# Normalising attention from PSUM: no copy on ScalarE, attention product eight units later, new unit tables

## The chip, the cores and the metric

One core of one Trainium2 chip runs the whole kernel. The metric is the device time of one execution in microseconds, the median of several runs. Engines: TensorE (PE, its weight loads PEld), VectorE (DVE), ScalarE (ACT), GpSimd (POOL) and SyncE (SP), which issues most DMAs.

## The reference

Eight sequences x of 512 tokens by 512 channels go through one post-norm block, all in float32.

```python
q = x @ Wq                # 16 heads of 32
k, v = x @ Wk, x @ Wv     # 4 heads of 32, each serves 4 query heads
attn = softmax(q @ k.T / sqrt(32))
x = layernorm(x + (attn @ v) @ Wo)
x_scale = max(abs(x)) / 127          # per token; weights likewise per output, int8
y = (round(x / x_scale) @ w_int8.T) * x_scale * w_scale + bias
x = layernorm(x + y)
```

## The kernel before

**Tiling.** A sequence (b, 8 of them) is a segment. Its attention is cut into 4 groups (i) of 4 heads, a group into 4 steps (kt, 128 keys each), a step into 4 units (j, one head each): 16 steps and 64 units a segment. The engines' programs all walk the same 64 units, and what else an engine does is put behind a unit by tables: MIDDLE for six segments, FIRST and LAST for the ends. An entry such as scale_dve=(9, 26, 43, 55) says behind which unit VectorE does scale_o for the group before (entry 0: the last group of the segment before). So the tables are the order of each engine's queue; they hold no times. Semaphores keep the engines apart.

**A unit.** TensorE makes transposed scores into one of two banks (scores_t, L382); ScalarE's exp (L612) reads them and writes probs. Scores in the other orientation run 24 units ahead (scores, L373) into s_bank; VectorE takes row maxima from them (L786). The maxima of a group are transposed (max_t, L419, into z_bank), negated and split by ScalarE (max_hi, L635) and VectorE (max_lo, L791), and SyncE stacks them by two DMAs (stack_max, L1100) as extra rows under q, so that the scores come out with the maximum subtracted; this must be there before the next group's first scores_t.

**A step.** pv (L397) multiplies probs with v into o_bank, accumulating over the four steps; the step before is done behind the second unit (PV_AT). exp waits for pv of four steps earlier, since probs has four slots. GpSimd adds the four steps' probs into prob_sum (add_probs, L1007), 12 additions of 128x512 a group.

**A group's end.** ScalarE copies o_bank, negated, to o_norm (o_evacuate, L621), which frees o_bank for pv by o_read. TensorE sums prob_sum over keys into z_bank (sums, L411). ScalarE makes the inverse r = exp(-ln z) (inverse, L627 and L629). VectorE does three operations: one_ish = z r (correct, L799), o_norm = o_norm r (scale_o, L804), o_norm = (one_ish - 2) o_norm (normalize, L810), a Newton step. correct_done frees z_bank for the next max_t.

**Beside it.** For the next segment: transposes of x and projections through front_bank, each split into a high part (ScalarE) and a low part (VectorE). For the segment before, per tile t of 128 tokens: o_norm is split (L640, L815), out_proj (L328) goes into tail_bank, then residual1 (L825), statistics, GpSimd's inverse deviation (inv_std, L1012 to L1017), normalize1 (L647), add_bias (L852), scale_of_x, round_x, a transpose (L454), ffn (L462) into the same tail_bank; then rescale (L860) to u, residual2 (L867) to z, statistics2, inv_std and normalize2 (L666) to u, which SyncE stores. u_done frees tail_bank for the next out_proj; rescale waits for the store of the tile before.

Behind the last unit come the last group's pv, its sums, and the last projection and FFN of all four tiles (LAST_TAIL).

Of the kernel before, what the change touches and what calls it, by code (L numbers as in the profile page):

```python
# [13 lines left out]
P = 128  # L14
# [28 lines left out]
PV_AT = 1  # L43
# [3 lines left out]

    front_pe={Q3: (0, 1, 3), 0: (5,), 1: (9,), 2: (13,), 3: (15,), K: (18, 20, 21), Q0: (24, 25, 26), V: (29, 31,
        32), VT: (34,), Q1: (36, 38), Q2: (43, 44, 47)},
    front_act={Q3: 3, 0: 6, 1: 10, 2: 12, 3: 14, K: 21, Q0: 26, V: 32, VT: 34, Q1: 37, Q2: 50},  # L50
    front_dve={Q3: 3, 0: 7, 1: 11, 2: 13, 3: 15, K: 22, Q0: 28, Q1: 39, Q2: 50},
# [24 lines left out]
    round_act=(21, 33, 45, 57),
    xq_pe=(23, 35, 46, 58),
    xq_act=(23, 35, 46, 58),
    add_bias_dve=(22, 35, 45, 57),
    ffn_pe=(24, 36, 47, 60),  # L80
    rescale_dve=(24, 36, 47, 60),

    res2_dve=(24, 36, 48, 61),
    stats2_dve=(25, 36, 48, 62),
    rstd2_pool=(26, 36, 52, 63),
    norm2_act=(29, 44, 52, 63))
FIRST = dict(
    front_pe={Q3: (0, 1, 2, 3), 0: (6,), 1: (10,), 2: (12,), 3: (16,), K: (18, 19, 20), Q0: (23, 25), V: (29, 31,
        32), VT: (34,), Q1: (37, 39, 40), Q2: (43, 44, 47, 48)},
    front_act={Q3: 3, 0: 7, 1: 10, 2: 12, 3: 15, K: 20, Q0: 26, V: 32, VT: 34, Q1: 39, Q2: 49},  # L90
    front_dve={Q3: 4, 0: 9, 1: 11, 2: 13, 3: 16, K: 21, Q0: 27, Q1: 41, Q2: 49},
    sums_pe=(14, 22, 35, 51),
    inv_act=(15, 22, 35, 50),
    correct_dve=(19, 23, 37, 53),
    scale_dve=(21, 26, 44, 56),
    norm_dve=(22, 32, 46, 59),
    o_act=(1, 17, 34, 49),
    max_pe=(9, 25, 40, 56),
    max_hi_act=(9, 25, 39, 56),
    max_lo_dve=(10, 27, 39, 57))  # L100
LAST = dict(
    front_pe={Q3: (0, 1)},
    front_act={Q3: 2},
    front_dve={Q3: 4},
    sums_pe=(7, 22, 38, 55),
    inv_act=(7, 22, 39, 55),
    correct_dve=(9, 23, 42, 56),
    scale_dve=(9, 27, 42, 60),
    norm_dve=(9, 31, 42, 60),
    o_act=(3, 18, 36, 49),  # L110
    max_pe=(10, 25, 44, 60),
    max_hi_act=(10, 27, 44, 54),
    max_lo_dve=(10, 27, 44, 51),
    o_hi_act=(10, 20, 32, 40),
    o_lo_dve=(12, 22, 36, 47),
    wo_pe=((13, 14, 16), (26, 27, 28), (39, 40), (50, 51, 52)),
    load_sp=(18, 24, 42, 50),
    res1_dve=(16, 28, 41, 52),
    stats1_dve=(17, 29, 41, 52),
    rstd1_pool=(18, 31, 42, 55),  # L120
    norm1_act=(20, 32, 43, 55),
    maxx_dve=(20, 32, 43, 57),
    round_act=(21, 33, 45, 57),
    xq_pe=(22, 35, 46, 59),
    xq_act=(22, 35, 46, 59),
    add_bias_dve=(22, 34, 47, 57),
    ffn_pe=(24, 36, 47, 61),
    rescale_dve=(24, 36, 48, 61),
    res2_dve=(25, 37, 49, 62),
    stats2_dve=(26, 37, 55, 62),  # L130
    rstd2_pool=(29, 42, 57, 62),
    norm2_act=(29, 43, 57, 63))
# [1042 lines left out]
```

## Time and profile before

| | |
|---|---|
| median of 3 runs | 860.35 us (858.87 to 862.44) |
| profiled execution, its own time | 858.5 us |
| its span, first to last instruction | 856.7 us |
| TensorE busy | 774.4 us (90%) |
| VectorE busy | 698.3 us (82%) |
| GpSimd busy | 607.6 us (71%) |
| ScalarE busy | 494.5 us (58%) |
| mean granted TensorE clock | 0.958 |
| GpSimd's additions, L1007 | 344.2 + 170.3 us |

A busy share is that of an engine's execution; matmuls overlap each other and their ends are modelled, so TensorE's 90% is not 90% of its peak. Rows are written as: line, engine, operation, output<-inputs, shapes, count; then busy time, mean ns of one, and the idle time before them with what ended it. In rows in order of time the first number is the start in us from the span's beginning, the second how long, and [..] the idle time before it with its releaser. One row may join several equal operations (x8).

### The profile page before, as it was taken

The numbers are of one execution on the slowest core, as the hardware profiler recorded it, in microseconds if no ns is written. First come the engines' busy times: TensorE is split into PE (matmuls) and PEld (weight loads), VectorE is DVE, ScalarE is ACT, GpSimd is POOL, SyncE is SP. The second block draws the span as 40 slices with busy tenths as digits, with TensorE's granted clock in tenths as the row PEclk, the third lists the DMA queues.
The fourth block names the chain that finished last, engine by engine and source line by source line (L and its number), as shares of the span: only waits on it lengthen the run. The fifth ranks groups of instructions, "written<-read, shape, count | busy, mean of one in ns | idle before, by whom it ended". The sixth has DMA issues, their size and how long they took to land.

```text
span 856.7 us, 12297 instructions
## 1 busy us (share of the span) xinstructions
PE 774.4 (90%) x3752; PEld 431.5 (50%) x3752; DVE 698.3 (82%) x1131; ACT 494.5 (58%) x904; POOL 607.6 (71%) x673
## 2 busy tenths in 40 slices
PE   7698999899899998999899998999899998899874
PEld 5444554465456644565445654566445653344441
DVE  4689668789987898888988898878988789779667
ACT  3155566565566656666556556656666645556644
POOL 3365487687785878767876797957877877678935
PEclk9889899999999999999999999999999998889995
DMA  7531123042132223232231322322230421300001
GB/s 217 136 116 38 39 60 96 20 112 63 51 112 50 66 72 98 52 79 83 63 100 41 84 63 60 102 60 78 73 102 27 112 63 50 99 26 26 26 25 49
DMA packets 40897, 61.89 MB, mean 72 GB/s; under 512 B 10385, under 2 KB 12433, under 8 KB 40833
## 3 DMA queue, kind: packets, MB, share of 16 engines
q1 hardware_dynamic: 39488, 57.38, 24.3%
q0 software_dynamic: 1344, 3.74, 1.6%
q8 instruction: 30, 0.49, 0.3%
q14 instruction: 35, 0.28, 0.1%
HBM read 20.71 MB, written 8.39 MB: 34 GB/s over the span
## 4 chain that ended last, share of the span: by engine, by line
PE 48%; DVE 18%; issue 15%; POOL 12%; POOLq 3%; ACT 3%; DMA 1%; SPq 0%; DVEq 0%; ACTq 0%
POOL prob_sum L1007 10%; PE front_bank L328 9%; PE s_bank L373 8%; PE st_bank L382 8%; PE o_bank L397 8%; DVE row_max L786 7%; PE tail_bank L328 6%; DVE o_norm L810 3%; PE z_bank L411 2%; POOLq L1016 2%; PE front_bank L335 1%; DVE o_norm L804 1%; ACT probs L612 1%; PE tail_bank L462 1%; DVE one_ish L799 1%
## 5 line engine op out<-in xcount | busy, mean ns | idle before, releaser
L786 DVE TENSOR_REDUCE row_max<-s_bank 128x1 f32<-128x512 f32 x512 | 339.9, 681 | 84.7 <-PE s_bank L373 82.7
L612 ACT ACTIVATE probs<-st_bank 128x512 f32<-128x512 f32 x512 | 293.4, 595 | 190.7 <-PE st_bank L382 183.7
L1007 POOL TENSOR_TENSOR prob_sum<-prob_sum,probs 128x512 f32<-128x512 f32 x248 | 344.2, 1418 | 6.5 <-ACT probs L612 6.3
L382 PE MATMUL st_bank<-q_stack,k_stack 98*128 98x512 f32 x512 | 231.7, 454 | 9.9 <-ACT probs L612 6.2
L373 PE MATMUL s_bank<-k_stack,q_stack 96*128 96x512 f32 x512 | 214.2, 421 | 24.8 <-DVE row_max L786 23.4
L1007 POOL TENSOR_TENSOR prob_sum<-probs 128x512 f32<-128x512 f32 x128 | 170.3, 1356 | 66.7 <-PE z_bank L411 48.0
L382 PEld LDWEIGHTS st_bank<-q_stack,k_stack 98*128 98x128 f32 x512 | 98.5, 193 | 117.2 <-ACT probs L612 77.2
L397 PE MATMUL o_bank<-probs,v_tok 128*32 128x512 f32 x1024 | 143.1, 632 | 0.7 <-ACT probs L612 0.7
L373 PEld LDWEIGHTS s_bank<-k_stack,q_stack 96*128 96x128 f32 x512 | 99.8, 195 | 65.8 <-DVE row_max L786 35.4
L1012 POOL TENSOR_TENSOR rs<-mv,small 128x1 f32<-128x1 f32 x64 | 12.7, 198 | 124.4 <-DVE mv L830 124.4
L328 PE MATMUL tail_bank<-wo_hi,o_hi 128*128 128x512 f32 x112 | 45.9, 410 | 6.5 <-issue 6.5
L328 PE MATMUL front_bank<-x_lo,wq_hi 128*128 128x512 f32 x116 | 47.4, 408 | 0.0
L1015 POOL TENSOR_TENSOR rs<-rs,small 128x1 f32<-128x1 f32 x64 | 39.1, 611 | 11.3 <-issue 2.4
L328 PE MATMUL front_bank<-x_hi,wq_hi 128*128 128x512 f32 x116 | 46.4, 400 | 0.0
L328 PE MATMUL front_bank<-x_hi,wq_lo 128*128 128x512 f32 x116 | 46.3, 399 | 0.0
L328 PE MATMUL tail_bank<-wo_lo,o_hi 128*128 128x512 f32 x112 | 44.8, 400 | 0.0
L328 PE MATMUL tail_bank<-wo_hi,o_lo 128*128 128x512 f32 x112 | 44.4, 396 | 0.0
L397 PEld LDWEIGHTS o_bank<-probs,v_tok 128*32 128x32 f32 x1024 | 20.5, 109 | 46.1 <-issue 39.5
L810 DVE SCALAR_TENSOR_TENSOR o_norm<-one_ish,o_norm 128x512 f32<-128x512 f32 x32 | 42.9, 1341 | 0.1
L815 DVE TENSOR_TENSOR o_lo<-o_norm,o_hi 128x512 fp32r<-128x512 f32 x28 | 36.0, 1284 | 4.2 <-ACT o_hi L640 4.2
L411 PE MATMUL z_bank<-prob_sum,ones 128*32 128x512 f32 x256 | 33.9, 602 | 0.3 <-POOL prob_sum L1007 0.3
L666 ACT ACTIVATE u_sb<-z_sb,rs 128x512 f32<-128x512 f32 x28 | 22.6, 809 | 20.0 <-POOL rs L1017 20.0
(193 smaller groups left out, 1041.2 us busy)
## 6 DMA issues: line engine op xcount, KB each, us to landing
q_stack<-q_parts SPq DMA_DIRECT2D x357, 64.0 KB, 2.0
x_tok<-in_L_attn_x SPq DMA_DIRECT2D x36, 256.0 KB, 3.8
y_sb<-in_L_attn_x SPq DMA_DIRECT2D x28, 256.0 KB, 2.8
out<-u_sb SPq DMA_DIRECT2D x28, 256.0 KB, 2.3
k_stack<-k_parts SPq DMA_DIRECT2D x90, 64.0 KB, 2.0
probs<-in_L_attn_Wq SPq DMA_DIRECT2D x1, 1024.0 KB, 8.3
o_norm<-in_L_attn_Wo POOLq DMA_DIRECT2D x4, 256.0 KB, 7.6
q_stack<-neg_max SPq DMA_DIRECT2D x64, 8.0 KB, 1.8
```

What stands on the lines that cost most here:

```text
L328: last = nc.tensor.matmul(dst, left(c), right(c), start=(n == 0), stop=(n == PASSES - 1))
L373: nc.tensor.matmul(s_bank[:, qt % 2, :], q_stack[0:STACK, i, j, qt * P:(qt + 1) * P], k_stack[0:STACK, p, j, :], start=True, stop=True).th ...
L382: nc.tensor.matmul(st_bank[:, j % 2, :], k_stack[0:STACK_M, p, j, kt * P:(kt + 1) * P], q_stack[0:STACK_M, i, j, :], start=True, stop=True ...
L397: last = nc.tensor.matmul(o_bank[rows, :], v_tok[:, p, kt, rows], probs[:, kt, j, :], start=(kt == 0), stop=(kt == QT - 1), skip_group_che ...
L411: last = nc.tensor.matmul(z_bank[j * HEAD:(j + 1) * HEAD, :], ones[:, 0:HEAD], addend[:, j, :], start=(n == 0), stop=(n == len(addends) - ...
L612: nc.scalar.activation(probs[:, kt, j, :], st_bank[:, j % 2, :], ACT.Exp, scale=SCALE).then_inc(exp_done, 1)
L666: nc.scalar.activation(w["u"], w["z"], ACT.Identity, bias=rs2[:, t, 2:3], scale=rs2[:, t, 1:2]).then_inc(out_done, 1)
L786: nc.vector.tensor_reduce(row_max[:, i % 2, j * QT + qt:j * QT + qt + 1], s_bank[:, qt % 2, :], AX_X, ALU.max).then_inc(max_done, 1)
L810: nc.vector.scalar_tensor_tensor(out=o_norm[:, p, i, :], in0=one_ish[:], scalar=2.0, in1=o_norm[:, p, i, :], op0=ALU.subtract, op1=ALU.mul ...
L815: nc.vector.tensor_tensor(o_lo[:], o_norm[:, p, :, t * P:(t + 1) * P], o_hi[:].bitcast(F32), ALU.subtract).then_inc(o_lo_done, 1)
L1007: nc.gpsimd.tensor_tensor(prob_sum[:, j, :], first, probs[:, kt, j, :], ALU.add).then_inc(sum_done, 1)
L1015: nc.gpsimd.tensor_tensor(rs[:, t, 1:2], rs[:, t, 0:1], small[:, 0:1], ALU.pow)
```

## The change

- o_evacuate and o_read are gone. scale_o reads o_bank and frees it by scaled_done, for which pv now waits.
- correct writes -z r back into z_bank; normalize reads z_bank, (z_bank + 2) o_norm. one_ish is gone; max_t waits for norm_done.
- rescale writes back into the tile's bank, residual2 reads it there; out_proj waits for residual2 (z2_done). The wait for the store moves from rescale to normalize2 on ScalarE.
- pv of step n stands behind unit 4n + 13 and no longer 4n + 5. Three pv instead of one follow the last unit.
- All three tables are new; in MIDDLE the sums go from (7, 23, 37, 52) to (7, 23, 39, 55), and correct, scale_o and normalize follow in three units in a row.

```diff
-PV_AT = 1
+PV_STEPS, PV_LAG = 1, 13
...
-    sums_pe=(7, 23, 37, 52),
-    inv_act=(7, 24, 38, 53),
-    correct_dve=(9, 25, 40, 54),
-    scale_dve=(9, 26, 43, 55),
-    norm_dve=(11, 33, 44, 59),
-
-    o_act=(3, 17, 36, 52),
-
-    max_pe=(10, 27, 42, 55),
-    max_hi_act=(10, 27, 42, 56),
-    max_lo_dve=(10, 27, 42, 59),
...
+    sums_pe=(7, 23, 39, 55),
+    inv_act=(7, 23, 40, 55),
+    correct_dve=(8, 24, 41, 56),
+    scale_dve=(9, 25, 42, 57),
+    norm_dve=(10, 26, 43, 58),
+    max_pe=(11, 27, 44, 60),
+    max_hi_act=(11, 27, 44, 59),
+    max_lo_dve=(11, 27, 44, 59),
...
                 if kt == 0:
-                    wait(pe, o_read, b * GROUPS + i)
+                    wait(pe, scaled_done, b * GROUPS + i)
...
-                wait(pe, correct_done, b * GROUPS + i - 1)
+                wait(pe, norm_done, b * GROUPS + i - 1)
...
-                    pe.wait_ge(u_done, FREE + b * QT + t)
+                    pe.wait_ge(z2_done, FREE + b * QT + t)
...
-                    if j == PV_AT and s > 0:
-                        pv(b, p, s - 1)
-                    if j == PV_AT and s == 0 and tail:
-                        pv(b - 1, 1 - p, STEPS - 1)
+                    for first in range(0, STEPS, PV_STEPS):
+                        for n in range(first, first + PV_STEPS):
+                            if u == first * NKV + PV_LAG:
+                                pv(b, p, n)
+                            if u + UNITS == first * NKV + PV_LAG and tail:
+                                pv(b - 1, 1 - p, n)
...
-            def o_evacuate(b, p, i):
-
-                act.wait_ge(pv_done, b * STEPS + (i + 1) * QT)
...
-                nc.scalar.mul(o_norm[:, p, i, :], o_bank, -1.0).then_inc(o_read, 1)
...
                 act.wait_ge(rs2_done, b * QT + t + 1)
+                if not is_last(b):
+                    act.wait_ge(out_stored, FREE + (b * QT + t) * 16)
...
-                nc.vector.tensor_tensor(one_ish[:], z_bank, inv_sum[:], ALU.mult).then_inc(correct_done, 1)
+                nc.vector.scalar_tensor_tensor(out=z_bank, in0=z_bank, scalar=-1.0, in1=inv_sum[:], op0=ALU.mult,
+                                               op1=ALU.mult).then_inc(correct_done, 1)
...
-                dve.wait_ge(o_read, b * GROUPS + i + 1)
+                dve.wait_ge(pv_done, b * STEPS + (i + 1) * QT)
...
-                nc.vector.tensor_tensor(o_norm[:, p, i, :], o_norm[:, p, i, :], inv_sum[:], ALU.mult).then_inc(scaled_done, 1)
...
+                nc.vector.tensor_tensor(o_norm[:, p, i, :], o_bank, inv_sum[:], ALU.mult).then_inc(scaled_done, 1)
...
-                nc.vector.scalar_tensor_tensor(out=o_norm[:, p, i, :], in0=one_ish[:], scalar=2.0, in1=o_norm[:, p, i, :],
-                                               op0=ALU.subtract, op1=ALU.mult).then_inc(norm_done, 1)
+                nc.vector.scalar_tensor_tensor(out=o_norm[:, p, i, :], in0=z_bank, scalar=2.0, in1=o_norm[:, p, i, :],
+                                               op0=ALU.add, op1=ALU.mult).then_inc(norm_done, 1)
...
-                if not is_last(b):
-                    dve.wait_ge(out_stored, FREE + n * 16)
-                nc.vector.scalar_tensor_tensor(out=w["u"], in0=w["bank"], scalar=x_scale[:, t, 1:2],
+                nc.vector.scalar_tensor_tensor(out=w["bank"], in0=w["bank"], scalar=x_scale[:, t, 1:2],
...
-                nc.vector.tensor_tensor(w["z"], w["u"], w["z"], ALU.add).then_inc(z2_done, 1)
+                nc.vector.tensor_tensor(w["z"], w["bank"], w["z"], ALU.add).then_inc(z2_done, 1)
```

## Rows read from the trace of the kernel before

**Rows 1.** Windows: busy us (x) of PE, PEld, DVE, ACT, POOL; clock, DMA share, GB/s.

```profile
335.00:433.00 98.00, 92.47 (x464) 52.24 (x463) 83.97 (x136) 60.26 (x111) 74.86 (x80) 0.98 0.27 74
```

**Rows 2.** The page's part 4: shares of the chain that ended last.

```profile
PE 48%; DVE 18%; issue 15%; POOL 12%; POOLq 3%; ACT 3%; DMA 1%; SPq 0%; DVEq 0%; ACTq 0%
POOL prob_sum L1007 10%; PE front_bank L328 9%; PE s_bank L373 8%; PE st_bank L382 8%; PE o_bank L397 8%; DVE row_max L786 7%; PE tail_bank L328 6%; DVE o_norm L810 3%; PE z_bank L411 2%; POOLq L1016 2%; PE front_bank L335 1%; DVE o_norm L804 1%; ACT probs L612 1%; PE tail_bank L462 1%; DVE one_ish L799 1%
```

**Rows 3.** Chain in order of time (start us, us, what): one piece, twice.

```profile
384.44 5.92 POOL prob_sum L1007 x4
...
483.00 5.91 POOL prob_sum L1007 x4
```

**Rows 4.** Waits: who waited for whom, total us, times, longest us.

```profile
DVE row_max L786 <- PE s_bank L373: 82.7, 120, 3.9
...
PEld st_bank L382 <- ACT probs L612: 77.2, 100, 1.7
...
PEld s_bank L373 <- DVE row_max L786: 35.4, 60, 1.4
```

**Rows 5.** Operations by form, VectorE: busy us, mean ns, idle before.

```profile
L810 DVE SCALAR_TENSOR_TENSOR o_norm<-one_ish,o_norm 128x512 f32<-128x512 f32 x32 | 42.9, 1341 | 0.1
...
L804 DVE TENSOR_TENSOR o_norm<-o_norm,inv_sum 128x512 f32<-128x512 f32 x32 | 30.4, 951 | 0.0
...
L867 DVE TENSOR_TENSOR z_sb<-u_sb,z_sb 128x512 f32<-128x512 f32 x28 | 23.6, 842 | 0.5
...
L799 DVE TENSOR_TENSOR one_ish<-z_bank,inv_sum 128x512 f32<-128x512 f32 x32 | 21.8, 681 | 5.8 <-ACT inv_sum L629 5.7
...
L860 DVE SCALAR_TENSOR_TENSOR u_sb<-tail_bank,x_scale,w_scale 128x512 f32<-128x512 f32 x28 | 20.7, 740 | 8.1 <-PE tail_bank L462 8.1
```

**Rows 6.** GpSimd's additions: by form, then in order of time.

```profile
L1007 POOL TENSOR_TENSOR prob_sum<-prob_sum,probs 128x512 f32<-128x512 f32 x248 | 344.2, 1418 | 6.5 <-ACT probs L612 6.3 <-issue 0.2
...
375.66 2.53 POOL L1007 TENSOR_TENSOR prob_sum<-probs 128x512 f32<-128x512 f32 x2
```

**Rows 7.** VectorE in order of time, one batch: start us, us, operation.

```profile
349.12 1.57 DVE L810 SCALAR_TENSOR_TENSOR o_norm<-one_ish,o_norm 128x512 f32<-128x512 f32 x1
...
374.29 0.68 DVE L804 TENSOR_TENSOR o_norm<-o_norm,inv_sum 128x512 f32<-128x512 f32 x1
...
405.00 1.81 DVE L810 SCALAR_TENSOR_TENSOR o_norm<-one_ish,o_norm 128x512 f32<-128x512 f32 x1
...
411.95 1.14 DVE L867 TENSOR_TENSOR z_sb<-u_sb,z_sb 128x512 f32<-128x512 f32 x1
...
421.87 1.59 DVE L804 TENSOR_TENSOR o_norm<-o_norm,inv_sum 128x512 f32<-128x512 f32 x1
...
428.13 1.18 DVE L810 SCALAR_TENSOR_TENSOR o_norm<-one_ish,o_norm 128x512 f32<-128x512 f32 x1
```

**Rows 8.** Operations by form, ScalarE: the copy out of o_bank.

```profile
L621 ACT ACTIVATE o_norm<-o_bank 128x512 f32<-128x512 f32 x32 | 19.3, 602 | 3.7 <-PE o_bank L397 3.6
```

**Rows 9.** In order of time, one group's release: ScalarE, VectorE, TensorE.

```profile
345.26 0.63 ACT L629 ACTIVATE inv_sum<-inv_sum 128x512 f32<-128x512 f32 x1
...
347.08 0.68 DVE L804 TENSOR_TENSOR o_norm<-o_norm,inv_sum 128x512 f32<-128x512 f32 x1
...
349.91 1.06 PE L397 MATMUL o_bank<-probs,v_tok 128*32 128x512 f32 x8
```

**Rows 10.** In order of time, a batch's end: TensorE, SyncE's queue, TensorE.

```profile
422.10 0.27 PE L419 MATMUL z_bank<-ident,row_max 128*16 128x128 f32 x1 [1.61 <-DVE row_max L786]
...
428.23 1.15 SPq L1100 DMA_DIRECT2D q_stack<-neg_max  x2
...
431.56 0.39 PE L382 MATMUL st_bank<-q_stack,k_stack 98*128 98x512 f32 x1
```

**Rows 11.** In order of time, behind the last unit: TensorE, ScalarE.

```profile
820.76 1.06 PE L397 MATMUL o_bank<-probs,v_tok 128*32 128x512 f32 x8 [0.69 <-ACT probs L612]
...
824.31 0.57 ACT L621 ACTIVATE o_norm<-o_bank 128x512 f32<-128x512 f32 x1
```

More of the change, by code:

```diff
@@ new lines @@
+    max_pe=(9, 28, 43, 60),
+    max_hi_act=(10, 27, 44, 59),
+    max_lo_dve=(11, 28, 43, 59))
+LAST = dict(
+    front_pe={Q3: (0, 3)},
+    front_act={Q3: 3},
+    front_dve={Q3: 3},
+    sums_pe=(6, 22, 38, 54),
+    inv_act=(7, 23, 39, 55),
+    correct_dve=(8, 24, 40, 55),
+    scale_dve=(10, 25, 42, 57),
+    norm_dve=(10, 25, 42, 60),
+    max_pe=(12, 28, 44, 56),
+    max_hi_act=(12, 28, 43, 59),
+    max_lo_dve=(12, 28, 44, 60),
+    o_hi_act=(11, 16, 34, 40),
+    o_lo_dve=(11, 22, 36, 52),
+    wo_pe=((13, 14, 16), (26, 27, 28), (39, 40), (49, 51, 52)),
+    load_sp=(11, 19, 39, 51),
+    res1_dve=(16, 27, 41, 53),
+    stats1_dve=(16, 28, 41, 53),
+    rstd1_pool=(18, 30, 42, 55),
+    norm1_act=(19, 30, 42, 56),
+    maxx_dve=(19, 31, 42, 57),
+    round_act=(22, 33, 45, 57),
+    xq_pe=(22, 35, 46, 59),
+    xq_act=(22, 34, 46, 59),
+    add_bias_dve=(20, 35, 46, 60),
+    ffn_pe=(23, 36, 46, 62),
+    rescale_dve=(23, 36, 47, 62),
+    res2_dve=(23, 37, 49, 63),
+    stats2_dve=(26, 37, 55, 63),
+    rstd2_pool=(29, 41, 58, 63),
+    norm2_act=(31, 41, 57, 63))
@@ L406, in sums @@
                 apart = is_last(b) and i == GROUPS - 1
+                if apart:
+                    pe.wait_ge(norm_done, B * GROUPS - 1)
                 pe.wait_ge(sum_done, (b * GROUPS + i) * ADDS + ADDS - (2 * NKV if apart else 0))
@@ L439, in last_out_proj @@
                     else:
-                        pe.wait_ge(u_done, FREE + (B - 1) * QT)
+                        pe.wait_ge(z2_done, FREE + (B - 1) * QT)
                 pe.wait_ge(last_hi_done, end)
@@ L542, in _ @@
             segment(B - 1, 1, front=False, tail=True)
-            pv(B - 1, 1, STEPS - 1)
+            for first in range(0, STEPS, PV_STEPS):
+                for n in range(first, first + PV_STEPS):
+                    if first * NKV + PV_LAG >= UNITS:
+                        pv(B - 1, 1, n)
             sums(B - 1, GROUPS - 1)
@@ L671, in segment @@
                     exp(b, u)
-                    if u in plan["o_act"]:
-                        i = plan["o_act"].index(u)
-                        if i or tail:
-                            o_evacuate(*before(b, p, i))
                     if u in plan["inv_act"]:
@@ L734, in _ @@
             segment(B - 1, 1, front=False, tail=True)
-            o_evacuate(B - 1, 1, GROUPS - 1)
             inverse(B - 1, GROUPS - 1)
@@ L864, in residual2 @@
                 w, n = buffers(b, t), b * QT + t
-                dve.wait_ge(u_done, FREE + n + 1)
+                dve.wait_ge(u_done, n + 1)
                 dve.wait_ge(xb_done, FREE + n + 1)
-                nc.vector.tensor_tensor(w["z"], w["u"], w["z"], ALU.add).then_inc(z2_done, 1)
+                nc.vector.tensor_tensor(w["z"], w["bank"], w["z"], ALU.add).then_inc(z2_done, 1)
             def statistics2(b, t):
-                dve.wait_ge(z2_done, b * QT + t + 1)
+                dve.wait_ge(z2_done, FREE + b * QT + t + 1)
                 statistics(t, buffers(b, t)["z"], mv2, mv2_done)
@@ L949, in _ @@
             nc.vector.memset(ones[:], 1.0).then_inc(consts_set, 1)
-            for n, freed in enumerate((u_done, wo_done, xb_done, out_done, out_stored, xqt_done)):
+            for n, freed in enumerate((z2_done, wo_done, xb_done, out_done, out_stored, xqt_done)):
                 nc.vector.memset(freed_mark[:, n:n + 1], 0.0).then_inc(freed, FREE)
```

93 lines of the change are left out of this document (28 added, 65 removed).

## The prediction

> **What bounds the kernel now.** I read the windows of a middle stretch first, then the chain that ended last, then the waits, then single operations in order of time. In a stretch of 98 us VectorE's execution is busy for 84 us, TensorE for 92, GpSimd for 75, ScalarE for 60 [rows 1]. The chain goes 48% through TensorE, 18% through VectorE, 12% through GpSimd [rows 2]; three groups of VectorE that the change touches stand in it: L810 with 3%, L804 and L799 with 1% each. The same piece of the chain comes back after 98.56 us [rows 3], so a batch costs 98.6 us and a unit of the plan (64 in a batch) 1.54 us. Six of the eight batches are of this kind.
>
> The engines hold each other by two pairs of banks. VectorE's row maxima wait 82.7 us for TensorE's scores, TensorE's scores wait 35.4 us at the weight load for the row maxima [rows 4]: neither is the bound throughout. The chain is TensorE's where projections run and VectorE's where an attention group is normalised. So VectorE's time counts only in the stretches where it is full, and there it counts in full.
>
> **What VectorE's normalising costs now.** L799 reads PSUM and one SBUF tensor and takes 681 ns in the mean; L804, with two inputs in SBUF, 951; L810, two in SBUF, 1341; L867 842 [rows 5]. The spread shows why. At 374.29 L804 took 0.68 us [rows 7], done before GpSimd's next additions began at 375.66 [rows 6]; L804 at 421.87 took 1.59, L810 at 349.12, 405.00 and 428.13 took 1.57, 1.81 and 1.18, L867 at 411.95 1.14 [rows 7], all while additions ran. GpSimd pays too: two additions in a quiet moment take 2.53 us, 1.27 each, the mean is 1.42 [rows 6]. L799 and L860 have one input in PSUM, and their means are 681 and 740 although GpSimd adds most of the time. I read this as: two SBUF inputs on VectorE collide with GpSimd's additions, one SBUF and one PSUM input do not.
>
> **The change, part by part.**
>
> Normalising. scale_o, normalize and residual2 each get one PSUM input. Priced by L799: L804 saves 951 - 681 = 270 ns x 32 = 8.6 us; L810 saves 660 x 32 = 21.1; L867 saves 842 - 681 = 161 x 28 = 4.5. Together 34 us of VectorE. correct becomes a scalar_tensor_tensor that writes PSUM; no row has a VectorE operation with a PSUM output. Its bounds: the 681 of L799 (nothing) and the 740 of L860, also a scalar_tensor_tensor with a PSUM input (60 ns x 32 = 2 us more); the same 60 ns may fall on normalize, and on rescale, which now also writes PSUM. I take 2 us in all, 0 to 5 for the range; a gain is excluded, since no 512-wide VectorE row of this kind is below 0.67. Net 32 us of VectorE.
>
> How much lies on the path: in the batch of rows 7 the lengthened operations stand where VectorE has next to no idle time. The excess over the undisturbed 0.68 is 0.89 + 1.13 + 0.46 + 0.91 + 0.50 = 3.9 us a batch (349.12, 405.00, 411.95, 421.87, 428.13). That is the upper end. The lower is the chain's own share of L810, 3% or 26 us [rows 2], of which 660 of 1341 ns are excess: 13 us, 1.6 a batch. I take 3.2, nearer the upper end, because the operations beside the chain stand in the same full stretches: 3.2 x 6 = 19 us, and 3 us for the first and the last batch together. 22 us.
>
> GpSimd. The additions' excess is (1418 - 1270) ns x 248 = 37 us [rows 6]. Five lines of VectorE with two SBUF inputs cause it; three of the five go, so I take half, 18 us of GpSimd. Additions are 10% of the chain [rows 2], 86 us of the 514 us that L1007 is busy, so 18 x 86/514 = 3 us.
>
> ScalarE. The 32 copies L621 of 602 ns go, 19 us [rows 8]. ScalarE is busy 60 of 98 us and the copy is in none of the chain's lines: nothing, but for the end: there the copy starts at 824.31 in front of the logarithm (L627) [rows 11], some 0.5 us on the path.
>
> The lag. PV of step n moves from unit 4n + 5 to 4n + 13; same matmuls, no cost on TensorE. It must move: o_bank is now freed by scale_o, which needs the inverse, and no longer by a plain copy. **The added wait** is TensorE's on scaled_done ahead of a group's first PV; behind it are the next scores of both kinds, so exp and the maxima starve with it. Its cover: the inverse starts 345.26 and ends 0.6 later, scale_o started 347.08 and ended 347.76, and the PV that stands in unit 13 ran at 349.91 [rows 9]: 2.1 us. In the other groups the plan leaves four units, about 6 us, less the sums' shift by two or three units. I take nothing; without cover it is the slower rival. exp's wait for PV of four steps before shrinks from 11 units to 3; the scores order covers that.
>
> The z bank. max_t now waits for norm_done, with correct, scale_o and normalize in three units in a row (8, 9, 10) and max_t in 11: as tight as correct 9 and max_t 10 was. But correct follows the sums by a single unit (55, 56) where there were two. Within it come sums, Ln and Exp, some 1.1 + 1.25 us, so VectorE stands up to 0.8 us with row maxima queued behind. One such stall a batch in a stretch where VectorE is full: 0.8 x 6 = 5 us lost. The fourth max_t moves from unit 55 to 60: before, it held TensorE 1.61 us for a row maximum at 422.10 [rows 10], beside a full VectorE, so I book no gain. After it the stacking DMAs of SP have four units: they were issued at 428.23 and the next batch's first transposed score ran at 431.56 [rows 10]; VectorE's max_lo has not moved (59), so the cover stays a few tenths. Its price if gone, 0.5 us a batch, 3 us, is in the range.
>
> FFN. out_proj waits for z2_done instead of u_done, one VectorE operation later, two units ahead of its use; normalize2 waits for the store of the tile before, which stands at least six units (9 us) back. Nothing for both. SP, ScalarE and GpSimd keep their order but for the plan's small shifts.
>
> The end. Two more PVs stand behind the last unit, 1.06 us each [rows 11]; one of them fits into the wait of 0.69 us ahead of PV at 820.76. About 1.4 later, less the 0.5 of the copy: 1 us lost.
>
> **A price from the notes.** L799, from PSUM, and L804 undisturbed, from SBUF, take 681 and 680 ns [rows 5, 7]. The Trainium skill ("VectorE: DVE Perf Modes", section "The TRN2 errata") gives VectorE 120 cycles of fixed cost with a PSUM source and 58 with an SBUF source, and its "Rules for kernel authors" advise to copy to SBUF first if many operations follow. By that, an estimate, each of 92 moved reads would cost 65 ns more, 6 us of VectorE; this trace has no such difference.
>
> **Sum.** 22 + 3 - 5 - 1 - 1 (what of the dearer forms is on the path) = 18 us. The profiled execution took 858.5 us, 856.7 its span and 1.8 around it: 840.5. The median of the three runs is 860.35, 1.85 above it: **842.3**.
>
> **The rivals.**
> - More than that (chance 0.08). TensorE idles 5.5 us in 98 [rows 1], 33 us over six batches, and with the first and last some 40; if every hold-up comes from VectorE's lengthened operations, 860.35 - 40 = 820. Against: ScalarE's exp holds TensorE's weight loads for 77.2 us [rows 4], more than the maxima do.
> - Absorbed (0.14). The VectorE stretches get shorter, but TensorE, exp or GpSimd's additions, which are serial with waits for the statistics, end at nearly the same time. Then only what the chain has beyond them goes, 0 to 4 us: 858. For it: 92 of 98 us busy on TensorE. Against: modelled ends make that 92 too high, and at 420 to 432 TensorE waits.
> - The release chain (0.10), slower. sums, Ln, Exp, correct, row maximum, scale_o become serial with TensorE. If sums come late, because GpSimd's twelve additions do, TensorE stands at each of the 31 first PVs. The saved 18 us are used up at 0.6 us each; at 1 us 842.3 + 31 = 873. It decides from the point where scale_o ends more than 2.1 us later against unit 13 than in rows 9.
> - PSUM reads are dearer in the mix (0.05): 60 ns (L860 - L799) on 92 reads, 5.5 us of VectorE, 3.5 on the path: 846. By the Trainium skill's 65 ns (above) the time would be the same, 846.
>
> **How the numbers follow.** The forecast has 0.63 (832 to 854). Faster by over 0.5% (below 856.05; half a per cent is about what a measurement of this kernel can tell from no change) is forecast, more and PSUM: 0.76. Same 0.14, slower 0.10. The range goes from 826, which cuts off the case of more, to 859, which cuts off the slower one.
>
> **What would show it.** Right: VectorE's scale and normalize at 0.68 to 0.74 with no tail to 1.8; additions at 1.42 fall to about 1.35; batches of 95 to 96 us; VectorE busy 4 us less a batch. Wrong: TensorE's o_bank matmuls wait for scaled_done by tenths of a us a group (release chain); VectorE's idle time before correct grows over 1 us a group; a VectorE operation with PSUM output at over 0.8 us. The prediction fails upward if batches stay at 98 us although VectorE is less busy.

## The result, and the profile after

The changed kernel takes 878.79 us (median of four executions, 871.33 to 880.66) against 860.49 us for the kernel before on the same chip (858.87 to 862.44): a ratio of 1.0195, with a 95% interval of 1.0132 to 1.0259. Forecast were 842.3 us and a range of 826 to 859. It is slower, not faster; in a second sitting (b_again below) it can't be told from the kernel before, 1.0038 with an interval of 0.9977 to 1.0100, and it is never the forecast gain. A ratio compares only executions within 1.5% of the fastest of the same kernel, so for b_again, e_shift and f_form it leaves out the longest ones, while the medians are over all. The profiled execution took 871.33 us, 869.5 of them its span; before, 858.5 and 856.7.

The operations that the change was about did what was forecast. VectorE by form after (busy us, mean ns of one, idle before; answers to [rows 5]; of the two last lines here, those of before follow):

```profile
L802 DVE TENSOR_TENSOR o_lo<-o_norm,o_hi 128x512 fp32r<-128x512 f32 x28 | 47.9, 1710 | 0.1
L839 DVE TENSOR_TENSOR z_sb<-xn_sb,bias 128x512 f32<-128x512 f32 x28 | 35.7, 1275 | 0.2 <-ACT u_sb L652 0.2
L780 DVE SCALAR_TENSOR_TENSOR z_bank<-z_bank,inv_sum 128x512 f32<-128x512 f32 x32 | 22.1, 690 | 7.8 <-ACT inv_sum L613 7.8
L797 DVE SCALAR_TENSOR_TENSOR o_norm<-z_bank,o_norm 128x512 f32<-128x512 f32 x32 | 21.8, 680 | 0.2
L791 DVE TENSOR_TENSOR o_norm<-o_bank,inv_sum 128x512 f32<-128x512 f32 x32 | 21.7, 679 | 0.0
L845 DVE SCALAR_TENSOR_TENSOR tail_bank<-tail_bank,x_scale,w_scale 128x512 f32<-128x512 f32 x29 | 21.7, 749 | 9.5 <-PE tail_bank L450 9.4
...
L852 DVE TENSOR_TENSOR z_sb<-tail_bank,z_sb 128x512 f32<-128x512 f32 x28 | 19.2, 686 | 0.7
```

And of the kernel before, the same view, two lines that the change leaves alone and on which the prediction did not rest:

```profile
L815 DVE TENSOR_TENSOR o_lo<-o_norm,o_hi 128x512 fp32r<-128x512 f32 x28 | 36.0, 1284 | 4.2 <-ACT o_hi L640 4.2
...
L852 DVE TENSOR_TENSOR z_sb<-xn_sb,bias 128x512 f32<-128x512 f32 x28 | 28.2, 1006 | 0.7 <-ACT u_sb L666 0.7
```

scale_o went from 951 to 679 ns, normalize from 1341 to 680, residual2 from 842 to 686, 34 us of VectorE together. But two lines that still have both inputs in SBUF grew: o_split_lo from 1284 to 1710, add_bias from 1006 to 1275, 19.4 us together. GpSimd's additions got cheaper, 1418 to 1327 ns [rows 6]:

```profile
L992 POOL TENSOR_TENSOR prob_sum<-prob_sum,probs 128x512 f32<-128x512 f32 x248 | 321.7, 1327 | 2.6 <-ACT probs L605 2.0
```

The chain that ended last looks different from that of before [rows 2]: it goes through GpSimd's additions and through issue, no longer through TensorE (part 4 of the page of after):

```profile
issue 31%; PE 25%; POOL 24%; DVE 7%; POOLq 6%; ACT 5%; DMA 2%; SPq 1%; DVEq 0%; ACTq 0%
```

What TensorE waited for (total us, times, longest us), after:

```profile
PE tail_bank L314 <- issue: 21.8, 6, 5.3
PE z_bank L407 <- DVE o_norm L797: 10.3, 15, 1.2
PE s_bank L359 <- DVE row_max L767: 10.2, 17, 1.8
PE st_bank L368 <- DMA q_stack<-neg_max: 6.7, 7, 3.3
```

The first line leads to the loss. The out projection stood there for 6.5 us in all before, now for 21.8, up to 5.3 at once; "issue" is what the profile writes where it has no releaser. The operations in order of time show one. The mid-stretch of after, start us and us:

```profile
344.76 5.00 POOL L992 TENSOR_TENSOR prob_sum<-probs 128x512 f32<-128x512 f32 x4 [2.04 <-PE z_bank L399]
...
349.74 6.18 POOL L992 TENSOR_TENSOR prob_sum<-prob_sum,probs 128x512 f32<-128x512 f32 x5
...
351.30 5.17 DVE L802 TENSOR_TENSOR o_lo<-o_norm,o_hi 128x512 fp32r<-128x512 f32 x1
...
356.39 1.27 DVE L767 TENSOR_REDUCE row_max<-s_bank 128x1 f32<-128x512 f32 x2
356.57 0.76 PE L314 MATMUL tail_bank<-wo_hi,o_hi 128*128 128x512 f32 x1 [4.04 <-issue]
357.13 0.63 PE L314 MATMUL tail_bank<-wo_lo,o_hi 128*128 128x512 f32 x1
...
359.93 0.60 ACT L605 ACTIVATE probs<-st_bank 128x512 f32<-128x512 f32 x1 [5.79 <-PE st_bank L368]
...
361.13 0.39 PE L314 MATMUL tail_bank<-wo_lo,o_hi 128*128 128x512 f32 x1
```

GpSimd makes nine additions without a pause, 344.76 to 355.92, some 1.24 us each. VectorE's o_lo starts at 351.30, in the middle of one, and ends at 356.47, when the last one has ended. It was held over four additions: 5.17 us for an operation that takes 0.68 alone. GpSimd's next instruction waits 9 us for VectorE's statistics of the same tile, so the hold ends when GpSimd itself has to wait. Behind it on VectorE stand the row maxima; TensorE has a matmul of the out projection that needs o_lo next, and stands 4.04 us; exp on ScalarE waits 5.79. Then TensorE's matmuls take 0.63 us until 359.7 and 0.39 from 360.9 on: the granted clock behind TensorE's 4.04 us of standing was at the lower of its two levels (1.2 GHz; 0.50 of full in the view of windows, whose columns are those of [rows 1]) and then back at the higher (2.4 GHz):

```profile
356.50:359.70 3.20, 3.13 (x8) 2.48 (x9) 1.77 (x3) 0.00 (x0) 0.00 (x0) 0.50 0.00 0
360.00:363.00 3.00, 3.00 (x19) 2.29 (x21) 2.33 (x4) 2.05 (x4) 0.00 (x0) 1.00 0.00 0
```

Before, the same operation in the same place, in a row of eleven additions without a pause (344.62 to 359.73), took one collision's price:

```profile
351.81 1.80 DVE L815 TENSOR_TENSOR o_lo<-o_norm,o_hi 128x512 fp32r<-128x512 f32 x1
```

**What a hold costs.** I cut each trace at the first transposed score of each batch. Lengths in us, with a star where an o_lo took over 1.9 us. "Mended" is an experiment below, the changed kernel without the hold:

```
batch     0      1      2       3       4      5       6       7      head+tail
before   94.6   99.5   98.8    98.3    98.5   98.3   102.8    88.4    77
after    93.6   96.8  101.3*  100.3*   95.1  102.1*  102.4*   97.7*   80
mended   96.2   96.7   94.8    94.6    94.6   94.6    94.9    88.0    80
```

The two middle batches (1 to 6) without a star take 96.8 and 95.1 us, about as forecast ("batches of 95 to 96"). Each star costs 5.7 to 9.7 us against the mended kernel. For the one at 351.30 it is 5.7, of which 5.17 - 0.67 = 4.5 are the held operation; the other 1.2 is about what 3 us at half the clock can cost, but that part was not tested by itself. The five cost 36.9 us; all eight batches together differ by 34.9.

### The profile page after: what moved, and what is told of

It is laid out like the page before. It is cut to its first block, busy times and chain, and to the rows that moved or that the text cites. A ratio compares the mean times of both kernels' runs of the same rounds, so it can differ in the third digit from the quotient of the medians.

```text
span 869.5 us, 12234 instructions
## 1 busy us (share of the span) xinstructions
PE 778.9 (90%) x3723; PEld 438.9 (50%) x3752; DVE 684.2 (79%) x1131; ACT 477.0 (55%) x872; POOL 579.1 (67%) x673
## 4 chain that ended last, share of the span: by engine, by line
issue 31%; PE 25%; POOL 24%; DVE 7%; POOLq 6%; ACT 5%; DMA 2%; SPq 1%; DVEq 0%; ACTq 0%
POOL prob_sum L992 21%; PE s_bank L359 5%; PE st_bank L368 5%; PE o_bank L383 5%; PE front_bank L314 4%; POOLq L1001 4%; DVE row_max L767 4%; ACT probs L605 2%; POOLq L999 1%; DMA q_stack<-neg_max 1%; PE z_bank L399 1%; PE tail_bank L314 1%; POOL rs L1002 1%; PE st_bank L314 1%; POOL rs L998 1%
## 5 line engine op out<-in xcount | busy, mean ns | idle before, releaser
L992 POOL TENSOR_TENSOR prob_sum<-prob_sum,probs 128x512 f32<-128x512 f32 x248 | 321.7, 1327 | 2.6 <-ACT probs L605 2.0
L359 PE MATMUL s_bank<-k_stack,q_stack 96*128 96x512 f32 x512 | 214.1, 420 | 11.6 <-DVE row_max L767 10.2
L992 POOL TENSOR_TENSOR prob_sum<-probs 128x512 f32<-128x512 f32 x128 | 166.6, 1328 | 73.5 <-PE z_bank L399 57.5
L383 PE MATMUL o_bank<-probs,v_tok 128*32 128x512 f32 x1024 | 139.4, 619 | 0.0
L314 PE MATMUL tail_bank<-wo_hi,o_hi 128*128 128x512 f32 x112 | 49.5, 442 | 21.9 <-issue 21.8
L1000 POOL TENSOR_TENSOR rs<-rs,small 128x1 f32<-128x1 f32 x64 | 40.4, 632 | 11.3 <-issue 2.4
L802 DVE TENSOR_TENSOR o_lo<-o_norm,o_hi 128x512 fp32r<-128x512 f32 x28 | 47.9, 1710 | 0.1
L314 PE MATMUL tail_bank<-wo_lo,o_hi 128*128 128x512 f32 x112 | 47.5, 424 | 0.0
L383 PEld LDWEIGHTS o_bank<-probs,v_tok 128*32 128x32 f32 x1024 | 20.5, 109 | 45.8 <-issue 41.1
L314 PEld LDWEIGHTS tail_bank<-wo_hi,o_hi 128*128 128x128 f32 x112 | 22.9, 204 | 39.6 <-issue 35.1
L631 ACT ACTIVATE xn_sb<-y_sb,rs 128x512 f32<-128x512 f32 x28 | 22.8, 815 | 28.1 <-POOL rs L1002 28.1
L839 DVE TENSOR_TENSOR z_sb<-xn_sb,bias 128x512 f32<-128x512 f32 x28 | 35.7, 1275 | 0.2 <-ACT u_sb L652 0.2
```

The lines of the kernel that those rows point to most:

```text
L314: last = nc.tensor.matmul(dst, left(c), right(c), start=(n == 0), stop=(n == PASSES - 1))
L359: nc.tensor.matmul(s_bank[:, qt % 2, :], q_stack[0:STACK, i, j, qt * P:(qt + 1) * P], k_stack[0:STACK, p, j, :], start=True, stop=True).th ...
L383: last = nc.tensor.matmul(o_bank[rows, :], v_tok[:, p, kt, rows], probs[:, kt, j, :], start=(kt == 0), stop=(kt == QT - 1), skip_group_che ...
L631: nc.scalar.activation(w["xn"], w["y"], ACT.Identity, bias=rs1[:, t, 2:3], scale=rs1[:, t, 1:2]).then_inc(xn_done, 1)
L802: nc.vector.tensor_tensor(o_lo[:], o_norm[:, p, :, t * P:(t + 1) * P], o_hi[:].bitcast(F32), ALU.subtract).then_inc(o_lo_done, 1)
L839: nc.vector.tensor_tensor(w["z"], w["xn"], bias[:], ALU.add).then_inc(xb_done, 1)
```

## The experiments

Theory H (hold): the loss is tile 0's o_split_lo, held over several additions. Rivals: the z bank, whose transposed maxima wait for normalize (10.3 us above); and the plan of units, which the change moves in many places. All runs of whole kernels are compared with the kernel before on the same chip.

**b_again.** The changed kernel as it is, in the company of the others.

> The changed kernel unchanged, for a second trace and its spread. Theory one (VectorE's o_lo of a batch's first tile, two inputs in SBUF, is held for several of GpSimd's additions in a row): 871 to 881 us, and each batch with an o_lo of over 3 us lasts 100 to 102 us, one without 95 to 97; the time follows the number of such batches. Rival (the new waits on the z bank, max_t behind norm_done): the batches all have one length, near 100, whatever o_lo takes.

866.04 us (857.85 to 871.76), ratio 1.0038 [0.9977, 1.0100]. That is below the 871 to 881 that theory H had. Five holds in its trace again, in other batches (1, 2, 3, 5 and 6): these take 100.4 to 102.9 us, batch 4 without one 95.2, so the batches don't have one length and the z bank rival fails here. The loss is not a fixed number. Batch 1 is held here and not in the first trace, batch 7 the other way round; and with five holds each, the two profiled executions took 864.57 and 871.33 us. All eight executions lie between 857.85 and 880.66; how many holds the six without a trace had is not known.

**b_olo_psum ("mended").** ScalarE copies tile 0's slice into the free tail bank, and o_split_lo reads it from there; the other tiles stay as they are.

```
+ if t == 0: act.wait_ge(z2_done, FREE + b * QT)
+            nc.scalar.copy(<tail_bank>, o_norm[:, p, :, 0:P]).then_inc(o_copy_done, 1)
  ...
+ if t == 0: dve.wait_ge(o_copy_done, b + 1)
- nc.vector.tensor_tensor(o_lo[:], o_norm[...], o_hi[:], ...)
+ nc.vector.tensor_tensor(o_lo[:], <tail_bank> if t == 0 else o_norm[...], o_hi[:], ...)
```

> The first tile's o_lo reads o_norm from a copy that ScalarE puts into tail_bank, which is free then: one PSUM and one SBUF input, the same result, 0.6 us more of ScalarE a batch. Theory one: o_lo at 0.68 us in the first tile, no batch over 98 us, 850 us (the profiled 871 less about 20 us of held time), 1% faster than the kernel before. Rival (waits on the z bank): 870 or more, since nothing of them is changed.

833.55 us (827.5 to 836.32), ratio 0.9683 [0.9634, 0.9731]. By the ratios, 1.0038 and 0.9683 of 860 us, it gains 31 us on b_again by one operation a batch. The 850 expected took off the held time alone; the table above shows that a hold costs more than itself. The same place in its trace, start us and us:

```profile
341.85 3.74 POOL L998 TENSOR_TENSOR prob_sum<-probs 128x512 f32<-128x512 f32 x3
345.54 6.27 POOL L998 TENSOR_TENSOR prob_sum<-prob_sum,probs 128x512 f32<-128x512 f32 x5
...
347.12 0.67 DVE L808 TENSOR_TENSOR o_lo<-tail_bank,o_hi 128x512 fp32r<-128x512 f32 x1
```

The additions run on as before and o_lo takes 0.67 us in the midst of them. By form (x7 is tile 0, x21 the others):

```profile
L808 DVE TENSOR_TENSOR o_lo<-o_norm,o_hi x21: 676/683/1811, 163.9 to 776.7; 128x512 fp32r<-128x512 f32 x21
L808 DVE TENSOR_TENSOR o_lo<-tail_bank,o_hi x7: 669/669/692, 155.6 to 725.9; 128x512 fp32r<-128x512 f32 x7
```

(lowest, median, highest ns). add_bias stays at a mean of 1234 ns here, so its rise is no part of what the mend gives back. TensorE is busy 91.87 us of 95 in the mid-stretch at full clock, where after had 87.98 at 0.98 (windows 335 to 430, first mended, then after; columns as in [rows 1]):

```profile
335.00:430.00 95.00, 91.87 (x463) 52.13 (x466) 79.76 (x139) 58.88 (x110) 71.80 (x81) 1.00 0.28 78
```

```profile
335.00:430.00 95.00, 87.98 (x440) 50.53 (x441) 78.76 (x129) 55.63 (x102) 67.20 (x77) 0.98 0.28 76
```

**e_max_late.** The mended kernel, with the transposed maxima (max_t, its copy and max_lo) of the first two groups one unit later in the middle batches: max_pe, max_hi_act and max_lo_dve at 12 and 28 instead of 11 and 27.

> The mended changed kernel, with max_t, max_hi and max_lo of the first two groups one unit later (12, 28 for 11, 27) in the middle batches. If the new wait of max_t for norm_done (19 us of TensorE's weight loads) costs time: 3 to 8 us less than 833.6. If it is covered: 833 to 835; if the stacked maxima then come too late for the next group's scores: 837 to 845.

832.34 us (829.92 to 839.41), ratio 0.9686 [0.9623, 0.9749]. What TensorE waits for on normalize falls from 10.2 us to 4.8, and the time stays. The first line is that of the mended kernel, the second of this one:

```profile
PE z_bank L407 <- DVE o_norm L800: 10.2, 15, 0.9
```

```profile
PE z_bank L407 <- DVE o_norm L800: 4.8, 9, 0.8
```

The wait on the z bank is new and real, but half of it gone brings no time that could be told from noise (some 7 us by the two intervals): it does not make the loss, and the rival falls. That holds while normalize is short; c_norm_two below shows it otherwise.

**before_olo_psum.** The kernel before with the same mend (the copy waits on u_done there).

> The kernel before, with the first tile's o_lo reading ScalarE's copy in tail_bank. If the change's own worth is what the forecast had (18 us, path time of normalising), this kernel gains only what its own o_lo had over 0.68 us, 1.1 us in each of seven batches: 853 to 857, and stays 18 to 22 us behind the changed kernel with the same mend (833.6). Rival: the mend alone makes the 26 us, then this one too is at 835.

852.43 us (849.07 to 853.15), ratio 0.9901 [0.9867, 0.9934]. With tile 0's o_lo mended on both sides, the change is worth 852.43 - 833.55 = 18.9 us, give or take some 5 by the two intervals. The prediction's sum was 18.

**c_norm_two.** The mended kernel, with correct writing SBUF again and normalize reading it there; scale_o, residual2, the lag and the plan stay as changed.

```
- nc.vector.scalar_tensor_tensor(out=z_bank, in0=z_bank, ...)        # correct
+ nc.vector.scalar_tensor_tensor(out=one_ish[:], in0=z_bank, ...)
- nc.vector.scalar_tensor_tensor(out=o_norm[...], in0=z_bank, ...)    # normalize
+ nc.vector.scalar_tensor_tensor(out=o_norm[...], in0=one_ish[:], ...)
```

> The mended changed kernel with one part of the change undone: correct writes to SBUF (one_ish), and normalize reads two SBUF inputs. Forecast's term for normalize: 660 ns x 32 = 21 us of VectorE, 10 to 15 us of it on the path, so 844 to 849 against 833.6. Rival (VectorE is covered by TensorE now): 834 to 837, or less than 4 us.

855.14 us (854.38 to 861.03), ratio 0.9961 [0.9929, 0.9992]: slower than the mended kernel by 21.6 us. normalize is back at 1245 ns:

```profile
L801 DVE SCALAR_TENSOR_TENSOR o_norm<-one_ish,o_norm x32: 679/1250/1834, 88.9 to 824.0; 128x512 f32<-128x512 f32 x32
```

That is (1245 - 680) x 32 = 18 us of VectorE, and the time pays all of it and more: 855.14 is above the 844 to 849 expected, and I had taken 3.2 of 3.9 us as on the path. TensorE's waits show by which way. On normalize at the z bank it stands 26.6 us, where the mended kernel had 10.2:

```profile
PE z_bank L408 <- DVE o_norm L801: 26.6, 22, 2.1
```

More goes with TensorE's clock. Batches 2 and 3 of this run as windows (the last numbers but two are the granted clock, 0.98 and 1.00):

```profile
239.40:337.80 98.40, 92.78 (x461) 52.21 (x465) 81.68 (x138) 58.71 (x109) 72.81 (x80) 0.98 0.27 74
337.80:434.60 96.80, 91.22 (x460) 51.80 (x465) 81.57 (x138) 58.64 (x109) 72.85 (x80) 1.00 0.27 75
```

VectorE's work is the same in both. Batches 1, 2, 4 and 5 each have some 3 us at the lower level beside a wait for normalize, and 2, 4 and 5 take 98.3 to 98.4 us; 3 and 6 have none and take 96.8 and 97.0. The mended kernel has no such stretch in its six middle batches. The 21.6 is the price in the changed plan, where correct, scale_o and normalize stand in three units in a row with the maxima behind. It is not what normalize cost before: the whole change is worth only 18.9. How the gain divides between the other lines and the plan was not measured.

**d_norm_two.** The same edit on the changed kernel without the mend.

> The changed kernel unmended, with normalize on two SBUF inputs again. If the quieter GpSimd queue (additions no longer pushed back by normalize) is what lets o_lo be held, the holds go: no o_lo over 2 us and 844 to 852, faster than the change without this step back. If the place of o_lo and its ready additions are enough, the holds stay: 875 to 890.

858.51 us (851.38 to 860.83, ten executions), ratio 0.9980 [0.9955, 1.0005]. No hold: tile 0's o_lo takes at most 1.00 us. So the branch "the holds go" came true, at a time above its 844 to 852. Putting the collision of normalize back, worth 21.6 us, costs nothing against the changed kernel, because it takes the holds away. In six of its seven batches normalize, itself lengthened by an addition, ends 2.13 us ahead of o_lo; in the kernel before, where no o_lo was held either, it ends 1.12 us ahead in six of seven. That this collision is what lets o_lo through, and not the moment that it shifts (o_lo begins 1.03 us into an addition here, 0.32 in the changed kernel), was not tested apart; in b_olo_late below it begins 0.91 and 1.20 us into one and is held.

**b_drain.** Has GpSimd's lack of a pause to do with it? One line behind each addition:

```
+ pool.drain()
```

> A drain behind each of GpSimd's additions, so that the next one is not handed over while the last still runs. Theory one: the hold needs additions that follow without a gap; no VectorE operation over 2 us is left. The gap costs 0.05 to 0.2 us an addition of GpSimd, 2 to 10 us a batch of an engine that is not full: 850 to 865. If the hold stays with the drain, back-to-back hand-over is not what makes it. Rival (z bank): 875 to 885.

850.72 us (849.6 to 853.33), ratio 0.9896 [0.9859, 0.9933]. The additions now come some 1.50 us apart with a pause of 0.22 between, and no o_lo takes over 1.64:

```profile
348.29 1.29 POOL L992 TENSOR_TENSOR prob_sum<-prob_sum,probs 128x512 f32<-128x512 f32 x1 [0.22 <-POOL prob_sum L992]
349.79 1.29 POOL L992 TENSOR_TENSOR prob_sum<-prob_sum,probs 128x512 f32<-128x512 f32 x1 [0.22 <-POOL prob_sum L992]
```

```profile
L802 DVE TENSOR_TENSOR o_lo<-o_norm,o_hi x28: 675/846/1634, 148.4 to 790.4; 128x512 fp32r<-128x512 f32 x28
```

So with a drain and its 0.22 us of pause VectorE gets in. An addition takes a place of 1.50 us in the row instead of 1.24, some 0.26 x 376 = 98 us of GpSimd at most, an estimate, since many additions wait anyway; part of it and the ordinary collisions of tile 0's o_lo are on the path (850.72 against 833.55).

**b_olo_late, e_shift, f_form.** Is it the moment at which o_lo starts, or its operands? In the first, o_lo of tile 0 goes one unit later in the six middle batches (o_lo_dve 12 to 13, out_proj 14 to 15). In the second, a reduction of 64 columns (0.20 us) stands ahead of it. In the third it keeps its place but subtracts two other SBUF tensors, contiguous ones (w_scale - bias); this leaves out the low part of tile 0's out projection.

> The first tile's o_lo stands one unit later (13 for 12), its projection one unit later (15 for 14), in the six middle batches. Theory one: another phase against GpSimd's additions, so o_lo is let in after at most one addition (under 1.9 us) in most batches: 850 to 860. If o_lo is held whenever additions stand ready, whatever the phase: 870 to 880 as before. Rival (z bank): 870 to 880.

> The changed kernel unmended; VectorE does one more 64-wide reduction (about 0.2 us) ahead of the first tile's o_lo, nothing else. Held o_lo began 0.313 to 0.322 or 0.911 to 0.918 us behind the start of the addition that ran; this one should begin about 0.5 behind. If the moment decides: no hold, batches of 95 to 96 us, 838 to 848. If the place decides (first tile, many additions ready): holds as before, 865 to 880.

> The changed kernel unmended; the first tile's o_lo is replaced by a subtraction of two other SBUF tensors (w_scale and bias, contiguous, same size), so the low part of this tile is left out and its projection is not the reference's. If the place decides, the holds of over 4 us stay and the time is 860 to 880. If o_lo's own operands (strided, just written by ScalarE and VectorE) decide: no hold, 845 to 852.

- b_olo_late: 880.66 us (874.25 to 881.83), ratio 1.0225 [1.0177, 1.0273], six holds.
- e_shift: 866.77 us (852.69 to 882.77, ten executions), ratio 0.9985 [0.9938, 1.0032]. The profiled one is among the two longest (882.67), with seven holds.
- f_form: 875.15 us (861.71 to 878.08, ten executions), ratio 1.0061 [1.0014, 1.0107], six holds.

```profile
357.11 0.20 DVE L803 TENSOR_REDUCE shift<-ones 128x1 f32<-128x64 f32 x1
357.23 5.04 DVE L805 TENSOR_TENSOR o_lo<-o_norm,o_hi 128x512 fp32r<-128x512 f32 x1
```

```profile
L803 DVE TENSOR_TENSOR o_lo<-w_scale,bias x7: 1203/5162/6661, 153.2 to 754.3; 128x512 fp32r<-128x512 f32 x7
```

The first fence is e_shift in order of time, the second f_form (lowest, median, highest ns). Held o_lo began 0.31 to 0.33, 0.43 to 0.44, 0.91 and 1.20 us into the running addition, in the last batch also 0.04 to 0.06 and 1.27; others that began 0.31, 0.63, 0.92 and 1.27 us into one were not held. So neither the moment within some tenths of a us nor the tensors decide it by themselves: with two SBUF inputs in this place of the changed kernel's batch, 29 of 35 were held. Counted over the twelve traces of whole kernels, an operation over 1.9 us being a hold:

```
operation                                      traces   seen   meet an addition   held
o_lo, tile 0: after, b_again, b_olo_late,         5       35          35            29
              e_shift, f_form
o_lo, tile 0: before, b_drain, d_norm_two         3       21          21             0
o_lo, tile 0, one input in PSUM                   4       28          28             0
o_lo, tiles 1 to 3                               12      252         110             0
add_bias                                         12      336         336             3
scale_o, normalize, residual2, on two SBUF        4      248         156             0
```

**micro, micro_drain, micro_close, micro_long.** The meeting alone: only GpSimd's additions, VectorE's subtraction and a reduction of growing width ahead of it, which shifts the subtraction in small steps against the additions; nothing of the reference is computed. micro has 128 trials of six additions, micro_drain the drain behind each, micro_close 256 trials with the additions closer (1.22 us apart). micro_long has twelve additions with two waits each, eight reductions on VectorE ahead and ScalarE copying beside.

> The disputed cost by itself; the whole computation is left out, the output is x. 128 trials: GpSimd makes six additions of 128x512 in a row, all ready, and VectorE, after a reduction whose width grows by 10 elements a trial, one o_lo with two SBUF inputs. Theory one: in some of the phases o_lo is held to the end of the six additions (4 to 7 us), in the rest it is let in after the addition that runs (0.7 to 1.9 us, and the next addition takes 1.73 us). Rival (o_lo is slow for another reason, in the full kernel alone): no o_lo over 1.9 us in any trial.

> The same with a drain behind each addition. Theory one: no o_lo over 1.9 us in any of the 128 trials. Rival: as in the one without drain.

> The isolated additions again, now each waiting only for the addition four places back, as in the kernel, so that they follow at the kernel's distance of 1.22 to 1.25 us and not at 1.34. 256 trials, VectorE's start moved by 5 elements each; the whole computation is left out. Theory one, close hand-over lets GpSimd keep the port: a part of the trials has o_lo held to the end of the six additions, 4 to 7 us. Rival: closeness is not enough, no o_lo over 1.9 us.

> The isolated trial brought nearer to the kernel: twelve additions in a row, each with two waits, eight 512-wide reductions of VectorE one behind the other ahead of the moved one, and ScalarE copying all the while; 128 trials, the whole computation is left out. If a long undisturbed row of additions beside a busy VectorE is what lets GpSimd keep on, a part of the trials has o_lo over 1.9 us, up to the end of the twelve. If not, none has, and the condition stays open.

They ran 1142.52, 1221.79, 2120.76 and 2042.78 us, times that say nothing by themselves. The subtraction's ns (lowest, median, highest), micro_close and micro_long:

```profile
L207 DVE TENSOR_TENSOR o_lo<-o_norm,o_hi x256: 680/1197/1787, 39.5 to 2112.7; 128x512 fp32r<-128x512 f32 x128
```

```profile
L214 DVE TENSOR_TENSOR o_lo<-o_norm,o_hi x128: 680/1115/1773, 47.9 to 2031.5; 128x512 fp32r<-128x512 f32 x128
```

In 512 trials without a drain and 128 with one, the subtraction got in when the running addition ended, in six trials one addition later. It took 0.68 to 1.79 us, and the next addition paid too, 1.59 us in the mean in micro and 1.71 in micro_close. None of the trials is a hold, against theory one of micro and of micro_close. So a collision's ordinary price is what the prediction had seen, and a hold needs something of the whole kernel that these do not have. **What that is stays open.** Closeness of the additions, their number, their waits, reductions ahead and ScalarE's traffic beside were tried and are not enough; TensorE's and the DMA's work beside were not.

## Why the prediction was wrong

**The step that failed** is in "What VectorE's normalising costs now" and was carried into "GpSimd". I found that two SBUF inputs on VectorE collide with GpSimd's additions, and counted that "three of the five go". The two that stay, o_split_lo and add_bias, I took at no change or a relief, since there was less to collide with. Neither had a term, a bound or a rival. The longest of these operations in the trace of before took 1.86 us, and the sum had no room for a longer one; that was the ceiling only of that arrangement. Measured: o_split_lo's mean rose by 426 ns, tile 0's up to 5.17 and 6.67 us, and the five held batches took 36.9 us more than in the mended kernel, where the rest of the change gave 18.9. add_bias's mean rose by 269 ns, in the mended kernel by 228; that is inside the 18.9.

The holds as cause of the loss are shown: one operation taken off SBUF removes them and the loss (b_olo_psum), and the holds also go in two other ways (b_drain, d_norm_two). What in the full kernel lets GpSimd pass VectorE over several times stays open.

The Trainium skill ("SBUF — State Buffer", section "Who interferes with whom") says that a VectorE instruction with two SBUF inputs contends with a GpSimd instruction that reads SBUF, and calls the shared port pair "an exclusive lock". The traces agree on which forms collide (1.80 us on two SBUF inputs, 0.67 with one in PSUM). Read as one instruction waiting for one other, it would bound o_lo at some 0.68 + 1.25 us, an estimate; the 5.17 us over four additions are beyond that, and the measurement decides.

**Normalising: right.** 34 us of VectorE were forecast and 34 came. "2 us in all" for the dearer forms was 690 against 681 ns for correct and 749 against 740 for rescale: 0.5 us. A PSUM output costs next to nothing, and the rival of dearer PSUM reads is out with scale_o at 679 ns.

**GpSimd: right in size.** (1418 - 1327) x 248 = 23 us against 18.

**How much lies on the path: the sum right, its parts not tested one by one.** 18 forecast, 18.9 (some 5 either way) between the mended pair. c_norm_two shows that normalize's share passes in full in the changed plan, though by TensorE's wait at the z bank and by its clock, and not by VectorE being full. And one part the sum left out. Before, the fourth max_t of a batch held TensorE for a row maximum, 1.61 us at 422.10 [rows 10], "so I book no gain"; behind it the granted clock was mostly at the lower level (first line, 423 to 427). This wait was 10.4 us in all and is 0.8 in the mended kernel, over whose six middle batches the clock is full (last line); before_olo_psum has this wait in every one and stretches at the lower level in four of the six (second line, its six middle batches).

```profile
423.00:427.00 4.00, 4.00 (x18) 1.48 (x17) 3.88 (x8) 2.47 (x6) 4.00 (x3) 0.57 0.36 109
135.60:722.90 587.30, 554.28 (x2761) 315.70 (x2785) 498.24 (x820) 363.38 (x672) 446.09 (x476) 0.99 0.27 73
138.30:708.60 570.30, 548.42 (x2760) 310.98 (x2785) 475.81 (x821) 350.66 (x648) 427.84 (x477) 1.00 0.28 76
```

So some of the 18.9 belongs to this wait and to the clock, how much was not measured, and that the sum came out so close is in part luck.

**The lag: right.** The rival of the release chain (873) came close to the measured time by another way. TensorE's matmuls of o_bank wait for nothing, and their weight loads follow 45.8 us of idle time where it was 46.1 before, none of it put down to scaled_done:

```profile
L383 PE MATMUL o_bank<-probs,v_tok 128*32 128x512 f32 x1024 | 139.4, 619 | 0.0
```

Had I looked at the time alone, 871.33 in the profile against 873 would have confirmed a mechanism that isn't there.

**The z bank: wait right, price wrong.** correct's idle time rose from 5.8 to 7.8 us over 32 groups [rows 5], not by 5; half of TensorE's new wait of 10 us went without time to be seen (e_max_late), but with a long normalize this wait is where the time goes (c_norm_two).

**The end: right.** Behind the last batch after is 0.8 us longer, where 1 was booked. Ahead of the first it is 2.0 longer, but that head is 40.4 to 43.0 us long in the twelve traces of whole kernels and 40.4 in one of the changed ones too (b_drain), so it can't be put to the change.

**What was told to show it** held with its one exception: "scale and normalize at 0.68 to 0.74 with no tail to 1.8" and "batches of 95 to 96 us" came, and over the six middle batches VectorE is less busy by (498.24 - 475.81) / 6 = 3.7 us a batch between the mended pair (4 forecast). The batches of 95 to 96 are those without a hold. But the tail moved to an operation that the list did not name.

**A version that beats both** is the mended one: 833.55 us, or 832.34 with the maxima a unit later (no difference beyond noise), some 3% under the kernel before. Tile 0's o_lo should not read two SBUF tensors while GpSimd adds.

## What to carry to other kernels

When an edit takes a cost off some operations of a kind, list all that remain of the kind and give each a term and a rival; here one of the two that were left took back 22 to 37 us (the 18.9, and the 3 to 18 by which the changed kernel was above the kernel before in the two sittings), where the others gave 19. A row of operations without a pause on one engine can hold its partner to the end of the row, as in 29 of 35 cases here, so put an operation that must meet it on one PSUM input, or put it where the other engine waits. And where the profile names no releaser ("issue"), look in order of time for an operation several times as long as it is alone (here 5.17 us against 0.68), before believing the rival whose price happens to fit.

## What the runs showed of the hardware that was not expected

- VectorE's 128x512 subtraction on two SBUF tensors can be held over four additions of GpSimd (5.17 us) and, in the last batch of after, still longer (6.67 us). Each of the 29 ended 0.55 us behind the last addition of the row, when GpSimd came to a wait. A hold is not a fixed property of the program: of two traces of the same kernel, one has it in batch 1 and not in batch 7, the other the reverse.
- With a drain and a pause of 0.22 us between additions no hold is left (b_drain), and none is with a collision of another operation some 2 us ahead (d_norm_two; the shifted moment was not ruled out).
- The ordinary collision is paid on both sides: up to 1.1 us by VectorE, and the addition behind it takes 1.59 to 1.71 us in the mean instead of 1.26.
- TensorE's clock makes a hold dearer than it is: 4.04 us of standing were followed by matmuls of 0.63 instead of 0.39 us for some 3 us. In c_norm_two such a stretch is the difference between batches of 98.4 and 96.8 us with the same work of VectorE.
- scalar_tensor_tensor with a PSUM output takes 690 ns (constant scalar) and 749 (scalar from a tensor) at 128x512.
